# First attention by chunks of 64: the second chunk attends the first through a score block instead of a carried state

## Chip, cores and metric

One core of one Trainium2 chip. The metric is the device time of one execution in microseconds, lower is better.

## What is computed

Two layers over x of 16 sequences x 256 tokens x 128 features. Each layer normalizes the rows, runs an attention and a mixture of experts on them, and adds attention x silu(experts) to x. The change lies in the first attention, a gated linear attention with 4 heads, keys of 128 and values of 32, in chunks of 64 tokens:

```
G = cumsum(gk within a chunk)             # log gates, gk = log_sigmoid(..)/16
qg = q*exp(G)*scale ; k_intra = k*exp(-G) ; kg = k*exp(G_last - G)
A = tril(qg k_intra^T) ; o = A v          # inside a chunk
o += qg S ; S = S*exp(G_last) + kg^T v    # state carried to the next chunk
```

The output o is then divided by its root mean square per head, gated, and projected by Wo. The result of the attention multiplies that of the first experts later.

## The kernel before

The tokens are handled in 16 blocks b of 256, one sequence each. A sequence is laid out as two halves u of 128 columns, and its columns are ordered 63..0, 64..127 within a tile of 128 tokens (ORDER): chunk 0 of the tile runs backwards and chunk 1 forwards, and the gate sums start at their common border. So the two chunks of 64 of one tile share one reference point, and 128 tokens take part in one masked score block; only from the first 128 tokens to the second is something carried (the text calls these halves the first and the second chunk).

The work on a block is a pipeline of ticks t, written out by hand for every engine in `gla(t, part)` with part 0, 1, 2 (all five engines walk the same schedule, `walk`). In tick t block t gets its gates (`gate_out`, `gate_logs`, `gate_sigmoids`), block t-1 its exponentials (`decays`: ACT writes bufP and bufN, L1005 and L1006), values, queries and keys (`queries_keys` L501 to L503, `scaled` L1550 and L1552), block t-2 its scores, block t-3 its outputs (L551, L554), block t-4 its mean, gate and projection (`output_means` L559, `output_gates` L1922, `gated` L1558, `project` L567, `attended` L1045).

Ticks 1 to 6 run beside the scatter of the normalized rows to `xs` by GpSimd's indirect DMAs (L1877, 64 of them in 18 parts; each part waits for a product of TensorE that `part_multiplied` names) and the preparation of the expert weights (`w1`, L606, L607, L963, L1485). Then come 19 expert groups g of the first layer: `turn` (L616, L1082, L1589), the experts' up products (L661 to L663), tanh (`gates0`, L1093), product (`hidden0`, L1598), down product (`down0`, L675), bias (`biased0`, L1608) and indirect stores (L1896). TICKS says which group carries which tick: (7, 8, 9, 0, 10, 11, 0, 12, 13, 0, 14, 15, 0, 16, 0, 17, 18, 19, 0), 0 for none. A group runs: turn of group g+1, `gla(t, 0)`, experts parts 0 and 1, `gla(t, 1)`, down product, `gla(t, 2)`.

What each engine has in the parts that matter, in program order:

- TensorE part 0: `output_means(t-4)`, `gate_out(t)`, `key_values(t-3)` (L539). Part 1: `outputs(t-3)` from tick 7 on, `keys_turned(t-2)` (L517: four transposes of 128x128), `scores(t-2)` (L528, L529), `gate_in(t+1)` (L475), `values(t-1)` (L509). Part 2: `queries_keys(t-1)`, `project(t-4)`.
- ScalarE part 0: `outputs_scale` (L1039, L1041), `gate_logs` (L990 to L994). Part 1: `keys_moved(t-2)` (L1019), `decays(t-1)`, `gate_moved(t+1)` (L978), `values_moved(t-1)` (L1025). Part 2: `outputs_squared`, `chunk_hi`, `attended(t-4)`. Table loads are L881.
- VectorE part 0: `states(t-3)` (L1535), `gated`, the scan of `decays(t-1)` (L1514); before tick 7 the scan comes first. Part 1: `masked(t-2)` (L1527), `gate_low(t+1)` (L1496), `chunk_lo(t-1)` (L1518), `gate_sigmoids(t)` (L1505, L1506). Part 2: `scaled(t-1)`.
- GpSimd part 1: `chunk_ends(t-1)` (L1916), a 128x4 product that waits for both exponentials; and `output_gates(t-4)`, in part 0 from tick 7 on.

Before, the carried part goes: the scaled keys of the first 128 tokens are transposed on TensorE (`keys_turned`), copied out by ScalarE (`keys_moved`), multiplied with the values to a 128x32 state per head (`key_values`), scaled by `ends` on VectorE (`states`), and in `outputs` the state multiplies the queries of the second 128 tokens.

Matrix products go to a ring of four PSUM banks (`Ring`, `bank`): a product takes the next bank and first waits for the signal given for the bank's use four takes earlier. In a group with a tick the order of takes is: turn, state product, four for the experts (b0, a0, b1, a1), turned keys, two score banks, gate product, values, down product, four for queries and keys, projection. b0 and b1 are freed by the tanh rows, a0 and a1 by `hidden0`. An fp32 matmul shows as two records of the trace.

Of the kernel before, what the change touches and what calls it, by code (L numbers as in the profile page):

```python
# [68 lines left out]
def build(nc, A, out):  # L69
    with ExitStack() as ctx:  # L70
# [7 lines left out]
        def sig(name, per=1):  # L78
            return Sig(ctx.enter_context(nc.semaphore(name)), per)
# [55 lines left out]
        bufE = [sb(1040) for _ in range(2)]  # L135
        bufK, bufKT = [sb(1024) for _ in range(2)], [sb(512) for _ in range(2)]
        bufP, bufN = sb(1040), sb(1040)
# [3 lines left out]
        bufV = [sb(256) for _ in range(3)]  # L141
        bufS = [sb(128) for _ in range(2)]
        ends = [sb(4) for _ in range(4)]
        osq_all = sb(512)
# [101 lines left out]
        gate2, gate2_ln, decay = sig("gate2", 2), sig("gate2_ln", 4), sig("decay", 5)  # L246
        pn, p_ends = sig("exp_decay", 2), sig("chunk_ends")
# [3 lines left out]
        kt, kt_moved = sig("k_turned"), sig("k_turned_moved")  # L251
        att, att_masked = sig("att", 2), sig("att_masked", 2)
        kv, state = sig("kv"), sig("state")
        o_mm, o_sq, o_mean, o_rs, o_gate, o_y = sig("o_mm"), sig("o_squared"), sig("o_mean"), sig("o_rs", 2), sig("o_gate"), sig("o_gated")
# [134 lines left out]
        def _(eng):  # L389
# [121 lines left out]

            def keys_turned(b):
                k4 = bufK[b % 2].rearrange("p (h c) -> p h c", h=4)
                k = bank(("kt", b), kt_moved.at(b))
                eng.wait_ge(*qk_mul.at(b))
                for h in range(4):
                    i = eng.transpose(k[:, 128 * h:128 * h + 128], k4[:, h, 0:128], ident)  # L517
                i.then_inc(kt.sem, 1)

            def scores(b):  # L520

                q4 = bufQ[b % 3].rearrange("p (h c) -> p h c", h=4)
                k4 = bufK[b % 2].rearrange("p (h c) -> p h c", h=4)
                for u in range(2):
                    k, n = bank(("att", b, u), att_masked.at(b, u)), slice(128 * u, 128 * u + 128)
                    early, late = slice(128 * u, 128 * u + 64), slice(128 * u + 64, 128 * u + 128)
                    for h in range(4):
                        mm(k[0:64, 128 * h:128 * h + 128], k4[:, h, early], q4[:, h, n])  # L528
                        i = mm(k[64:128, 128 * h + 64:128 * h + 128], k4[:, h, late], q4[:, h, late])  # L529
                    i.then_inc(att.sem, 1)  # L530

            def key_values(b):

                KT, v = bufKT[b % 2], bufV[b % 3]
                k = bank(("kv", b), state.at(b))
                eng.wait_ge(*kt_moved.at(b))
                eng.wait_ge(*v_moved.at(b))
                for h in range(4):
                    i = mm(k[:, 32 * h:32 * h + 32], KT[:, 128 * h:128 * h + 128], v[:, 32 * h:32 * h + 32])  # L539
                i.then_inc(kv.sem, 1)  # L540

            def outputs(b):

                v, S, A4, o = bufV[b % 3], bufS[b % 2], bufAT[b % 2], o_banks[b % 2]
                q4 = bufQ[b % 3].rearrange("p (h c) -> p h c", h=4)
                if b > 1:
                    eng.wait_ge(*o_y.at(b - 2))
                for u in range(2):
                    eng.wait_ge(*att_masked.at(b, u))
                    for h in range(4):  # L550
                        mm(o[32 * h:32 * h + 32, 128 * u:128 * u + 128], v[:, 128 * u + 32 * h:128 * u + 32 * h + 32], A4[:, u, h, :], start=(u == 0), stop=(u == 0))  # L551
                eng.wait_ge(*state.at(b))
                for h in range(4):
                    i = mm(o[32 * h:32 * h + 32, 128:256], S[:, 32 * h:32 * h + 32], q4[:, h, 128:256], start=False)  # L554
                i.then_inc(o_mm.sem, 1)
# [14 lines left out]
            def gla(t, part):  # L570
                def at(b):
                    return 0 <= b < NB
                if part == 0:
                    if at(t - 4):
                        output_means(t - 4)
                    if at(t):
                        gate_out(t)
                    if at(t - 3):
                        key_values(t - 3)
                elif part == 1:  # L580
                    if at(t - 3) and t >= OUTPUTS_EARLY:
                        outputs(t - 3)
                    if at(t - 2):
                        keys_turned(t - 2)
                        scores(t - 2)
# [290 lines left out]
        def _(eng):  # L876
# [119 lines left out]
            def decays(b):  # L996
# [3 lines left out]
                if b >= 1:  # L1000
                    eng.wait_ge(*qk_mul.at(b - 1))
                    eng.wait_ge(*p_ends.at(b - 1))
                else:
                    eng.wait_ge(*set_pool.at(0, 11))
# [9 lines left out]

            def keys_moved(b):
                eng.wait_ge(*kt.at(b))
                if b >= 2:
                    eng.wait_ge(*kv.at(b - 2))
                act(bufKT[b % 2], bank_of["kt", b][:, :], ACT.Copy).then_inc(kt_moved.sem, 1)  # L1019

# [26 lines left out]
            def gla(t, part):  # L1047
# [7 lines left out]
                elif part == 1:  # L1055
                    if at(t - 2):
                        keys_moved(t - 2)
                    if at(t - 1):
# [216 lines left out]
        def _(eng):  # L1275
# [252 lines left out]

            def states(b):
                kv_, S = (a.rearrange("p (h d) -> p h d", h=4) for a in (bank_of["kv", b][:, 0:128], bufS[b % 2]))  # L1530
                eng.wait_ge(*kv.at(b))
                eng.wait_ge(*p_ends.at(b))
                if b > 1:
                    eng.wait_ge(*o_mm.at(b - 2))
                tt(S, kv_, bc(ends[b % 4], 2, [128, 4, 32]), ALU.mult).then_inc(state.sem, 1)  # L1535

# [23 lines left out]
            def gla(t, part):  # L1560
                def at(b):
                    return 0 <= b < NB
                if part == 0:
                    if at(t - 1) and t < OUTPUTS_EARLY:
                        decays(t - 1)
                    if at(t - 3):
                        states(t - 3)
                    if at(t - 4) and t >= OUTPUTS_EARLY:
# [14 lines left out]
                elif at(t - 1):  # L1583
                    scaled(t - 1)


# [200 lines left out]
        def _(eng):  # L1787
# [111 lines left out]
            def experts0(g, part):  # L1899
                if part == 0 and g >= 2:  # L1900
                    t = TICKS[g]
                    eng.wait_ge(*(kv.at(t - 3) if 0 < t < 19 else up[0].at(g, 1) if g < 18 else down[0].at(17)))
                    store(0, g - 2, 1)
                if part == 0 and g + 1 < GROUPS[0]:
                    ids(0, g + 1)
                if part == 2 and g >= 1:
                    store(0, g - 1, 0)
                    if g == 18:
                        store(0, 17, 1)

            def chunk_ends(b):
                P, N = (a.rearrange("p (h u s) -> p h u s", h=4, u=2) for a in (bufP, bufN))
                eng.wait_ge(*pn.at(b))
                if b >= 4:
                    eng.wait_ge(*state.at(b - 4))
                tt(ends[b % 4], P[:, :, 0, 128], N[:, :, 1, 64], ALU.mult).then_inc(p_ends.sem, 1)  # L1916

# [220 lines left out]
```

## Time and profile before

| | us |
|---|---|
| runs shown, median of 3 | 987.14 (986.79 to 999.11) |
| profiled execution, its own time | 995.33 |
| its span, first to last instruction | 993.3 |
| TensorE busy | 738.5 (74%) |
| VectorE busy | 646.1 (65%) |
| ScalarE busy | 616.1 (62%) |
| GpSimd busy | 453.9 (46%) |

Busy times are parts of the span and overlap each other. The rows below are of the profiled execution. Its time is 8 us above the median of the runs, so differences are to be taken against its own time. Ticks 1 to 6 lie between about 46 and 157 us of it, the groups with ticks 7 to 19 between 157 and 387 us; the rest, to 993 us, is the second layer, with the joining of the first.

### The profile page before, as it was taken

The page shows a single profiled execution, that of the slowest core. Times are in us where ns is not written, and L with a number is a line of the kernel's source. Part 1 is how long each engine was busy: PE and PEld are TensorE (multiplying, and loading weights), DVE is VectorE, ACT ScalarE, POOL GpSimd, SP SyncE. Part 2 cuts the span into 40 slices and gives each one's busy share as a digit, 9 for nine tenths or more (in the row PEclk, how much of TensorE's full clock was granted, in tenths as well). Part 3 has the DMA queues.
Part 4 walks back from the last instruction along what each step waited for, and adds up shares of the span by engine and source line. Part 5 has one row for each costly group of instructions (what it writes and reads, how often), then busy time and mean ns, then how long its engine had stood idle before and what let it go on. Part 6 is the DMA issues. An engine that isn't in the chain of part 4 may idle for free.

```text
span 993.3 us, 21325 instructions
## 1 busy us (share of the span) xinstructions
PE 738.5 (74%) x8182; PEld 573.3 (58%) x8182; DVE 646.1 (65%) x1190; ACT 616.1 (62%) x1139; POOL 453.9 (46%) x484
## 2 busy tenths in 40 slices
PE   6756776989898992466954788687978888888650
PEld 4535555878887892344642445456756766766540
DVE  5765655766666643777567554575677777687647
ACT  5653455766667462675641434475778878878775
POOL 4485763242443454100004665223566666756632
PEclk8777879999999996678885777698999999999985
DMA  9811222011111113400003321300111111110054
GB/s 310 304 45 47 62 64 58 20 50 31 47 47 39 46 42 108 115 1 2 1 1 119 121 85 60 86 13 23 30 39 41 34 39 39 42 36 26 19 158 118
DMA packets 62357, 63.81 MB, mean 64 GB/s; under 512 B 7378, under 2 KB 52322, under 8 KB 62132
## 3 DMA queue, kind: packets, MB, share of 16 engines
q1 hardware_dynamic: 53300, 44.02, 15.1%
q0 software_dynamic: 8960, 18.43, 5.7%
q8 instruction: 68, 1.11, 0.5%
q14 instruction: 29, 0.24, 0.1%
HBM read 31.88 MB, written 30.55 MB: 63 GB/s over the span
## 4 chain that ended last, share of the span: by engine, by line
PE 33%; ACT 19%; DVE 17%; issue 16%; POOL 9%; DMA 2%; another core or an unknown queue 2%; SPq 0%; ACTq 0%; POOLq 0%; DVEq 0%
POOL xs L1877 6%; ACT arena L1220 4%; PE bank L721 4%; ACT L881 3%; PE bank L786 3%; PE bank L675 3%; PE bank L798 2%; PE bank L528 2%; POOL ys L1896 2%; DVE arena L1644 2%; DVE arena L1737 2%; ACT arena L1121 2%; DVE arena L1624 1%; DVE arena L1642 1%
## 5 line engine op out<-in xcount | busy, mean ns | idle before, releaser
L1896 POOL DMA_INDIRECT ys<-arena x152 | 172.3, 1134 | 178.4 <-ACT arena L1149 56.3
L1877 POOL DMA_INDIRECT xs<-arena x128 | 131.3, 1026 | 77.1 <-issue 33.5
L1220 ACT ACTIVATE arena<-bank 128x512 f32<-128x512 f32 x192 | 99.1, 600 | 83.6 <-PE bank L786 62.1
L1737 DVE TENSOR_REDUCE arena<-bank 128x2 bf16<-128x512 f32 (+1 forms) x192 | 119.0, 682 | 41.9 <-PE bank L759 37.8
L661 PE MATMUL bank<-arena 128*128 128x128 bf16 x608 | 105.9, 220 | 6.4 <-DVE arena L1589 3.3
L662 PE MATMUL bank<-arena 128*128 128x128 bf16 x608 | 105.9, 220 | 0.0
L663 PE MATMUL bank<-arena 128*128 128x128 bf16 x608 | 105.9, 220 | 0.0
L881 ACT ACT_TABLE_LOAD x72 | 92.4, 1283 | 1.3
L1725 DVE SCALAR_TENSOR_TENSOR arena<-arena,bank 128x512 bf16<-128x512 bf16 x64 | 46.0, 746 | 71.2 <-ACT arena L1193 68.0
L721 PE MATMUL bank<-arena 128*128 128x256 f32 x256 | 67.2, 410 | 0.9 <-issue 0.9
L661 PEld LDWEIGHTS bank<-arena 128*128 x608 | 60.2, 99 | 9.6 <-issue 6.5
L662 PEld LDWEIGHTS bank<-arena 128*128 x608 | 59.8, 98 | 0.3
L663 PEld LDWEIGHTS bank<-arena 128*128 x608 | 59.6, 98 | 0.0
L1828 POOL TENSOR_TENSOR arena<-arena 128x4 f32<-128x4 f32 x16 | 16.2, 1010 | 87.9 <-DVE arena L1323 80.7
L721 PEld LDWEIGHTS bank<-arena 128*128 128x128 f32 x256 | 50.7, 208 | 9.3 <-issue 2.6
L691 PE MATMUL bank<-arena 128*128 x320 | 44.1, 296 | 14.5 <-POOL arena L1942 11.7
L1942 POOL TENSOR_TENSOR arena<-arena 128x1024 f32<-128x1024 f32 x19 | 44.7, 2355 | 20.4 <-ACT arena L1130 19.0
L691 PEld LDWEIGHTS bank<-arena 128*128 128x128 f32 x320 | 42.1, 211 | 17.5 <-issue 17.0
L756 PE MATMUL bank<-arena 32*128 32x256 bf16 (+1 forms) x512 | 22.8, 273 | 38.5 <-DVE arena L1725 14.9
L501 PE MATMUL bank<-arena 128*128 128x256 bf16 x128 | 37.9, 296 | 11.8 <-DVE arena L1518 7.5
L1193 ACT ACTIVATE arena<-bank 128x512 bf16<-128x512 f32 x64 | 36.6, 609 | 16.1 <-PE bank L721 15.6
L1937 POOL TENSOR_TENSOR arena<-arena 128x512 f32<-128x512 f32 x40 | 40.6, 1035 | 10.7 <-DVE arena L1644 10.7
(236 smaller groups left out, 2063.9 us busy)
## 6 DMA issues: line engine op xcount, KB each, us to landing
xs<-arena SPq DMA_DIRECT2D x19, 516.0 KB, 7.2
arena<-xs SPq DMA_DIRECT2D x38, 258.0 KB
arena<-ys SPq DMA_DIRECT2D x32, 256.0 KB, 5.1
arena<-in_MF SPq DMA_DIRECT2D x8, 512.0 KB
ys<-arena POOLq DMA_INDIRECT x152
arena<-in_x SPq DMA_DIRECT2D x8, 256.0 KB, 5.7
arena<-in_W SPq DMA_DIRECT2D x8, 256.0 KB
xs<-arena POOLq DMA_INDIRECT x128
```

The source lines that it names most:

```text
L661: mm(o, hi, b[:, 0, c4], stop=False)
L662: mm(o, hi, b[:, 1, c4], start=False, stop=False)
L663: i = mm(o, lo, b[:, 0, c4], start=False)
L691: i = mm(k[:, 128 * j:128 * j + 128], tb[g % 2][:, h0:h0 + 128], D, start=(c == 0), stop=(c == 1))
L721: j = mm(k[:, 256 * z:256 * z + 256], Wqk[:, c:c + 128], xnT[:, 256 * b:256 * b + 256])
L881: eng.preload_act_table_set(name)
L1220: act(PT[kt_][:, i, gs[0]:gs[0] + len(gs), :], bank_of["s2", b, n, i][:, :].rearrange("p (g q) -> p g q", q=w), ACT.Exp, scale=8 ** -0.5). ...
L1725: stt(T, hiT[n % 2], low_of[n // 2], bank_of["qk1", b, n][:, :], ALU.mult, ALU.add).then_inc(m_qk_moved.sem, 1)
L1737: red(negM[b % 2][:, u, 32 * i + gs[0]:32 * i + gs[0] + len(gs)], kv_, op=ALU.max, negate=True).then_inc(m_max.sem, 1)
L1877: eng.indirect_dma_start(xs[l][:, :], bass.IndirectOffsetOnAxis(ap=slot_i[l][:, m:m + 1], axis=0), xrow[:, t, :], None).then_inc(rows_move ...
L1896: eng.indirect_dma_start(ys[l][:, :], bass.IndirectOffsetOnAxis(ap=yid[g % 4][:, j:j + 1], axis=0), y[:, 128 * j:128 * j + 128], None).the ...
L1942: tt(T, T, U, ALU.mult).then_inc(f1_h.sem, 1)
```

## The change

`keys_turned`, `keys_moved`, `key_values`, `states` and `chunk_ends` go. Instead VectorE, behind `scaled(t-1)` in part 2, multiplies the keys of the first 128 tokens with `ends` (`keys_shifted`: a 128x4 product, then a 128x512 product into bufKX). TensorE multiplies them with the queries of the second 128 tokens to a third score bank, behind the two of `scores`; ScalarE copies it to bufX, where it copied the turned keys before; `outputs` multiplies it with the values. The scores inside a tile, formed before by two products of 64 keys (128 and 64 queries wide), are formed by one of 128 keys and 128 queries. The ring takes: the state product's bank is gone, and so is the turned keys'; the cross scores take one behind the score banks. ScalarE's exponentials wait for the new `ends` product instead of GpSimd's. The store on GpSimd that waited for the state product waits for `output_means(t-4)`.

```diff
-        bufK, bufKT = [sb(1024) for _ in range(2)], [sb(512) for _ in range(2)]
+        bufK, bufKX, bufX = [sb(1024) for _ in range(2)], [sb(512) for _ in range(2)], [sb(512) for _ in range(2)]
...
-        bufS = [sb(128) for _ in range(2)]
-        ends = [sb(4) for _ in range(4)]
+        ends = [sb(4) for _ in range(2)]
...
@@ TensorE
-            def keys_turned(b):
-                k4 = bufK[b % 2].rearrange("p (h c) -> p h c", h=4)
-                k = bank(("kt", b), kt_moved.at(b))
-                eng.wait_ge(*qk_mul.at(b))
-                for h in range(4):
-                    i = eng.transpose(k[:, 128 * h:128 * h + 128], k4[:, h, 0:128], ident)
-                i.then_inc(kt.sem, 1)
...
-                    early, late = slice(128 * u, 128 * u + 64), slice(128 * u + 64, 128 * u + 128)
+                    if u == 0:
+                        eng.wait_ge(*qk_mul.at(b))
                     for h in range(4):
-                        mm(k[0:64, 128 * h:128 * h + 128], k4[:, h, early], q4[:, h, n])
-                        i = mm(k[64:128, 128 * h + 64:128 * h + 128], k4[:, h, late], q4[:, h, late])
+                        i = mm(k[:, 128 * h:128 * h + 128], k4[:, h, n], q4[:, h, n])
                     i.then_inc(att.sem, 1)
-
-            def key_values(b):
-
-                KT, v = bufKT[b % 2], bufV[b % 3]
-                k = bank(("kv", b), state.at(b))
-                eng.wait_ge(*kt_moved.at(b))
-                eng.wait_ge(*v_moved.at(b))
+                k = bank(("cross", b), cross_moved.at(b))
+                eng.wait_ge(*k_shifted.at(b))
                 for h in range(4):
-                    i = mm(k[:, 32 * h:32 * h + 32], KT[:, 128 * h:128 * h + 128], v[:, 32 * h:32 * h + 32])
-                i.then_inc(kv.sem, 1)
+                    i = mm(k[:, 128 * h:128 * h + 128], bufKX[b % 2][:, 128 * h:128 * h + 128], q4[:, h, 128:256])
+                i.then_inc(cross.sem, 1)
...
+                eng.wait_ge(*v_moved.at(b))
                 for u in range(2):
...
-                eng.wait_ge(*state.at(b))
+                eng.wait_ge(*cross_moved.at(b))
                 for h in range(4):
-                    i = mm(o[32 * h:32 * h + 32, 128:256], S[:, 32 * h:32 * h + 32], q4[:, h, 128:256], start=False)
+                    i = mm(o[32 * h:32 * h + 32, 128:256], v[:, 32 * h:32 * h + 32], bufX[b % 2][:, 128 * h:128 * h + 128], start=False)
...
-                    if at(t - 3):
-                        key_values(t - 3)
...
-                        keys_turned(t - 2)
                         scores(t - 2)
@@ ScalarE
-                    eng.wait_ge(*p_ends.at(b - 1))
+                    eng.wait_ge(*k_shifted.at(b - 1, 0))
...
-            def keys_moved(b):
-                eng.wait_ge(*kt.at(b))
+            def crossed(b):
+                eng.wait_ge(*cross.at(b))
                 if b >= 2:
-                    eng.wait_ge(*kv.at(b - 2))
-                act(bufKT[b % 2], bank_of["kt", b][:, :], ACT.Copy).then_inc(kt_moved.sem, 1)
+                    eng.wait_ge(*o_mm.at(b - 2))
+                act(bufX[b % 2], bank_of["cross", b][:, :], ACT.Copy).then_inc(cross_moved.sem, 1)
...
-                        keys_moved(t - 2)
+                        crossed(t - 2)
@@ VectorE
-            def states(b):
-                kv_, S = (a.rearrange("p (h d) -> p h d", h=4) for a in (bank_of["kv", b][:, 0:128], bufS[b % 2]))
...
-                tt(S, kv_, bc(ends[b % 4], 2, [128, 4, 32]), ALU.mult).then_inc(state.sem, 1)
+            def keys_shifted(b):
+
+                k4, kx = (a.rearrange("p (h c) -> p h c", h=4) for a in (bufK[b % 2], bufKX[b % 2]))
+                P, N = (a.rearrange("p (h u s) -> p h u s", h=4, u=2) for a in (bufP, bufN))
+                tt(ends[b % 2], P[:, :, 0, 128], N[:, :, 1, 64], ALU.mult).then_inc(k_shifted.sem, 1)
+                eng.wait_ge(*k_shifted.at(b, 0))
+                eng.wait_ge(*qk_mul.at(b))
+                if b >= 2:
+                    eng.wait_ge(*cross.at(b - 2))
+                tt(kx, k4[:, :, 0:128], bc(ends[b % 2], 2, [128, 4, 128]), ALU.mult).then_inc(k_shifted.sem, 1)
...
-                    if at(t - 3):
-                        states(t - 3)
...
                     scaled(t - 1)
+                    keys_shifted(t - 1)
@@ GpSimd
-                    eng.wait_ge(*(kv.at(t - 3) if 0 < t < 19 else up[0].at(g, 1) if g < 18 else down[0].at(17)))
+                    eng.wait_ge(*(o_mean.at(t - 4) if t else up[0].at(g, 1) if g < 18 else down[0].at(17)))
...
-            def chunk_ends(b):
-                P, N = (a.rearrange("p (h u s) -> p h u s", h=4, u=2) for a in (bufP, bufN))
-                eng.wait_ge(*pn.at(b))
...
-                tt(ends[b % 4], P[:, :, 0, 128], N[:, :, 1, 64], ALU.mult).then_inc(p_ends.sem, 1)
...
-                if part == 1 and 0 <= t - 1 < NB:
-                    chunk_ends(t - 1)
```

## Rows read from the trace of the kernel before

**Rows 1.** By stage: window and its length, busy us of each engine, granted clock, DMA
```profile
46.00:157.00 111.00, 73.72 (x566) 54.04 (x566) 67.60 (x124) 52.62 (x89) 75.58 (x79) 0.77 0.17 53
157.00:387.00 230.00, 197.48 (x2430) 180.78 (x2430) 139.78 (x224) 146.91 (x226) 92.64 (x114) 0.95 0.15 42
```

**Rows 2.** Waits of 160 to 390 us: engine line, releaser, total us, times, longest
```profile
ACT arena L1045 <- PE bank L567: 35.4, 12, 4.2
```

**Rows 3.** TensorE in tick 9: start us, us, engine, line, operation, [idle before]
```profile
200.10 0.66 PE L517 MATMUL bank<-arena 128*128 128x128 f32 x4 [1.40 <-ACT arena L1093]
200.82 0.32 PE L528 MATMUL bank<-arena 128*64 128x128 f32 x1
...
202.71 0.66 PE L475 MATMUL bank<-arena 128*80 128x128 f32 x4
...
203.66 1.95 PE L675 MATMUL bank<-arena 128*128 128x128 f32 x16
205.44 0.27 PE L501 MATMUL bank<-arena 128*128 128x256 bf16 x1
...
208.06 0.61 PE L567 MATMUL bank<-arena 128*128 128x128 f32 x4
...
209.24 0.22 PE L661 MATMUL bank<-arena 128*128 128x128 bf16 x1
```

**Rows 4.** ScalarE in tick 9, the same columns
```profile
199.44 1.09 ACT L1093 ACTIVATE arena<-bank 128x512 f32<-128x512 f32 x2
200.79 0.60 ACT L1019 ACTIVATE arena<-bank 128x512 f32<-128x512 f32 x1 [0.26 <-PE bank L517]
...
203.41 0.38 ACT L978 ACTIVATE arena<-bank 80x256 bf16<-80x256 f32 x1
...
208.71 0.38 ACT L1045 ACTIVATE arena<-bank 128x256 f32<-128x256 f32 x1 [3.89 <-PE bank L567]
```

**Rows 5.** VectorE in tick 9
```profile
200.08 1.29 DVE L1598 SCALAR_TENSOR_TENSOR arena<-arena,bank 128x512 f32<-128x512 f32 x2 [1.60 <-ACT arena L1093]
...
203.82 0.42 DVE L1496 TENSOR_TENSOR arena<-bank,arena 16x256 bf16<-16x256 f32 x1 [0.26 <-ACT arena L978]
...
204.27 0.43 DVE L1518 TENSOR_TENSOR arena<-arena 128x256 bf16<-128x256 f32 x1
...
207.86 1.28 DVE L1552 TENSOR_TENSOR arena<-bank,arena 128x512 f32<-128x512 f32 x2
```

**Rows 6.** TensorE elsewhere: tick 7's first query product; tick 10's state product and turn
```profile
174.29 0.27 PE L501 MATMUL bank<-arena 128*128 128x256 bf16 x1 [1.03 <-DVE arena L1518]
...
215.13 0.98 PE L539 MATMUL bank<-arena 128*128 128x32 f32 x8
...
222.41 1.11 PE L517 MATMUL bank<-arena 128*128 128x128 f32 x4 [2.82 <-ACT arena L1093]
```

**Rows 7.** Granted clock in ticks 9 and 10, columns as in rows 1
```profile
200.10:205.40 5.30, 5.23 (x60) 4.83 (x61) 4.25 (x8) 4.29 (x8) 0.20 (x1) 1.00 0.22 50
222.40:230.40 8.00, 7.99 (x60) 7.33 (x61) 4.42 (x9) 4.90 (x9) 0.20 (x1) 0.63 0.15 35
```

**Rows 8.** Groups of 100 to 470 us: count, busy us, mean ns of one
```profile
L1535 DVE TENSOR_TENSOR arena<-bank,arena 128x128 f32<-128x128 f32 x15 | 4.4, 291 | 3.8 <-PE bank L539 2.7 <-issue 1.1
```

**Rows 9.** Lines L1673 and L1323: count, duration ns min/median/max, first and last start
```profile
L1673 DVE TENSOR_TENSOR arena<-arena x8: 681/684/685, 396.6 to 447.4; 128x512 f32<-128x512 f32 x8
...
L1323 DVE TENSOR_SCALAR arena<-arena x8: 160/163/382, 403.5 to 477.4; 128x4 f32<-128x4 f32 x8
```

**Rows 10.** GpSimd in the scatter stage: its wait in total, then rows in time
```profile
POOL arena L1916 <- ACT arena L1006: 12.2, 4, 5.2
...
154.75 0.95 POOL L1877 DMA_INDIRECT xs<-arena  x1 [0.30 <-issue]
```

**Rows 11.** TensorE where the scatter stage ends
```profile
155.73 0.38 PE L607 MATMUL bank<-arena 128*128 128x512 bf16 x1
160.57 2.04 PE L616 MATMUL bank<-arena 128*128 128x128 f32 x8 [4.46 <-DMA arena<-xs]
```

More of the change, by code:

```diff
@@ L246, in build @@
         gate2, gate2_ln, decay = sig("gate2", 2), sig("gate2_ln", 4), sig("decay", 5)
-        pn, p_ends = sig("exp_decay", 2), sig("chunk_ends")
+        pn, k_shifted = sig("exp_decay", 2), sig("k_shifted", 2)
         xq_hi, xq_lo = sig("chunk_hi"), sig("chunk_lo")
@@ L250, in build @@
         vv, v_moved = sig("v"), sig("v_moved")
-        kt, kt_moved = sig("k_turned"), sig("k_turned_moved")
+        cross, cross_moved = sig("att_cross"), sig("att_cross_moved")
         att, att_masked = sig("att", 2), sig("att_masked", 2)
-        kv, state = sig("kv"), sig("state")
         o_mm, o_sq, o_mean, o_rs, o_gate, o_y = sig("o_mm"), sig("o_squared"), sig("o_mean"), sig("o_rs", 2), sig("o_gate"), sig("o_gated")
@@ L525, in scores @@
                     k, n = bank(("att", b, u), att_masked.at(b, u)), slice(128 * u, 128 * u + 128)
-                    early, late = slice(128 * u, 128 * u + 64), slice(128 * u + 64, 128 * u + 128)
+                    if u == 0:
+                        eng.wait_ge(*qk_mul.at(b))
                     for h in range(4):
-                        mm(k[0:64, 128 * h:128 * h + 128], k4[:, h, early], q4[:, h, n])
-                        i = mm(k[64:128, 128 * h + 64:128 * h + 128], k4[:, h, late], q4[:, h, late])
+                        i = mm(k[:, 128 * h:128 * h + 128], k4[:, h, n], q4[:, h, n])
                     i.then_inc(att.sem, 1)
-            def key_values(b):
-                KT, v = bufKT[b % 2], bufV[b % 3]
-                k = bank(("kv", b), state.at(b))
-                eng.wait_ge(*kt_moved.at(b))
-                eng.wait_ge(*v_moved.at(b))
+                k = bank(("cross", b), cross_moved.at(b))
+                eng.wait_ge(*k_shifted.at(b))
                 for h in range(4):
-                    i = mm(k[:, 32 * h:32 * h + 32], KT[:, 128 * h:128 * h + 128], v[:, 32 * h:32 * h + 32])
-                i.then_inc(kv.sem, 1)
+                    i = mm(k[:, 128 * h:128 * h + 128], bufKX[b % 2][:, 128 * h:128 * h + 128], q4[:, h, 128:256])
+                i.then_inc(cross.sem, 1)
             def outputs(b):
-                v, S, A4, o = bufV[b % 3], bufS[b % 2], bufAT[b % 2], o_banks[b % 2]
-                q4 = bufQ[b % 3].rearrange("p (h c) -> p h c", h=4)
+                v, A4, o = bufV[b % 3], bufAT[b % 2], o_banks[b % 2]
                 if b > 1:
                     eng.wait_ge(*o_y.at(b - 2))
+                eng.wait_ge(*v_moved.at(b))
                 for u in range(2):
@@ L1527, in masked @@
                     eng.copy_predicated(bufAT[b % 2][:, u], bc(maskA, 1, [128, 4, 128]), bank_of["att", b, u].rearrange("p (h c) -> p h c", h=4)).then_inc(att_masked.sem, 1)
-            def states(b):
-                kv_, S = (a.rearrange("p (h d) -> p h d", h=4) for a in (bank_of["kv", b][:, 0:128], bufS[b % 2]))
[L1531 to L1534, printed above, removed]
-                tt(S, kv_, bc(ends[b % 4], 2, [128, 4, 32]), ALU.mult).then_inc(state.sem, 1)
+            def keys_shifted(b):
[7 more added lines that the diff above has]
+                tt(kx, k4[:, :, 0:128], bc(ends[b % 2], 2, [128, 4, 128]), ALU.mult).then_inc(k_shifted.sem, 1)
             def scaled(b):
@@ L1909, in experts0 @@
                         store(0, 17, 1)
-            def chunk_ends(b):
-                P, N = (a.rearrange("p (h u s) -> p h u s", h=4, u=2) for a in (bufP, bufN))
-                eng.wait_ge(*pn.at(b))
-                if b >= 4:
-                    eng.wait_ge(*state.at(b - 4))
-                tt(ends[b % 4], P[:, :, 0, 128], N[:, :, 1, 64], ALU.mult).then_inc(p_ends.sem, 1)
             def output_gates(b):
```

## The prediction, made before the run

> **What bounds the kernel now.** I read the time by stage first. The change touches the stretch up to 387 us and nothing behind it: the scatter stage (ticks 1 to 6, 46 to 157 us) and the expert groups with ticks 7 to 19 (157 to 387 us). In the second TensorE is busy 197.5 of 230 us, VectorE 140, ScalarE 147 [rows 1]: no engine is full, so the order of one tick decides. The waits say how: ScalarE stands 35.4 us, 12 times, before `attended` for the projection on TensorE [rows 2]. I then lined up one tick on three engines. In tick 9 ScalarE ends its first tanh at 199.44 + 0.60 = 200.04 [rows 4]; TensorE stood idle 1.40 us for it and then works without a gap: keys turned from 200.10, scores from 200.82, gate product 202.71, `down0` 203.66, queries and keys 205.44, projection 208.06 [rows 3]. ScalarE answers at 208.71, after 3.89 us idle [rows 4], and has its long row of gate logarithms before the next tanh. So the tick is a loop: a TensorE half (tanh to projection), then a ScalarE half (projection to tanh). A delay in either lengthens the tick; idle time of ScalarE inside the TensorE half is free, until it is used up.
>
> Inside the TensorE half runs a side chain that must be done before the queries: ScalarE's copy of the turned keys (200.79), two exponentials, the gate copy (203.41) [rows 4]; VectorE's `gate_low` (203.82) and `chunk_lo`, done at 204.27 + 0.43 = 204.70 [rows 5]. The queries start at 205.44 [rows 3]: the side chain has 0.7 us to spare, 0.6 after the 0.1 us that a wait takes. In tick 7, which has no `down0`, it has none: the queries there waited 1.03 us for VectorE [rows 6].
>
> **Part by part, per tick, at full clock.**
> TensorE. Scores: 16 records of 128x64 weights with the 128x64 ones beside them, 200.82 to 202.71, 1.9 us [rows 3]. Whole blocks are 16 records of 128x128 weights by 128 columns; `down0` issues 16 such in 1.78 us (203.66 to 205.44) [rows 3], 0.11 each. So the scores cost the same, since the two half-width products already ran side by side: between -0.1 and, if the halves had been worth something, +0.2; I take 0. The turn goes (200.10 to 200.76), and with it the gap until the scores; the cross scores come: 8 records, 0.9 us. The state product goes, 8 records from 215.13, 0.98 us [rows 6], but it lies in the ScalarE half, ahead of the 1.4 to 2.8 us that TensorE idles [rows 3, 6]: worth nothing there. The output products keep their count (v for the state, the moved cross scores for the queries): 0.
> ScalarE. A 128x512 copy for a 128x512 copy, 0.60 us both [rows 4]: 0. But the old copy waited for four turns, the new one waits for the scores and the cross scores. All three are queued behind the same tanh: first block 200.10 to 200.98 (its ring bank is now the one that the first tanh frees), second to 201.86 (bank free when VectorE's 0.69 us product ends, 200.77 from rows 5: no wait), cross to 202.74, last record's end about 202.9. The copy moves from 200.79 to 202.9: **+2.1 us**. Queued behind it on ScalarE are both exponentials and the gate copy; behind that on VectorE `gate_low`, `chunk_lo`, the sigmoids, all of `scaled`.
> VectorE. The state multiply goes, 0.29 us [rows 8]. Added: one 128x4 product, between 0.16 (a 128x4 operation) and 0.4, and one 128x512 product from the arena, 0.68 [rows 9]: 0.85 to 1.1, I take 0.9, net +0.6. It stands behind `scaled`, ahead of the next tick's `lo`, `gated` and scan, and VectorE idled 1.60 us for the tanh behind these [rows 5]. That wait hides it. If that cover were gone it would cost up to 0.6 x 10 = 6 us.
> The Trainium skill (SBUF — State Buffer, "Who interferes with whom") says that a VectorE instruction with both inputs in SBUF contends with a GpSimd instruction that reads SBUF, and that one blocks the other for its whole length; the new product has both inputs there, the state multiply had one in PSUM. By that rule some ticks would pay one more 0.7 us on VectorE. `chunk_lo` too has two such inputs and took 0.43 us in the row shown [rows 5], not stretched; GpSimd's reading operation is short and rare, so the sum leaves this out.
>
> Now the consequence. The side chain ends at 204.70 + 2.1 = 206.8 instead of 204.70; the queries start at 206.9 instead of 205.44: **+1.4 us** on the tick. VectorE's `scaled` is behind the side chain alone and moves the full 2.1: its end goes from 207.86 + 1.28 = 209.14 [rows 5] to 211.2. The next experts start at 209.24 [rows 3], because one of their ring banks is freed by that end. Where the next group has a tick, mean and gate products stand between (0.9 us) and cover the difference. Where it has none, the experts wait, and the loss is 2.1. Five ticks are of that kind (9, 11, 13, 15, 16), and tick 7 has no slack: 6 x 2.1 = 12.6. Ticks 8, 10, 12, 14: 4 x 1.4 = 5.6. In tick 10 the clock is 0.63 [rows 7] and everything on TensorE takes up to twice as long: the copy comes 4.1 us later, but ScalarE had idled 2 us there; about the same 1.2 to 1.4 remains. Sum **+18.2 us**. Ends of this term: if only TensorE's own surplus counted (0.9 + the shorter gap = 0.15 per tick) +1.5; if every tick paid 2.1 and the VectorE addition as well, 10 x 2.7 = +27. I take 18, since each step of it stands in rows.
> Tick 18: no exponentials; the state product there is on the chain: -0.8.
> GpSimd. `chunk_ends` and its wait for the exponentials go. In the groups nothing there is late. In the scatter stage it held up the scatters for 12.2 us [rows 10]. Without it the scatters run until the next of their own waits (gate, value and query products, `output_gates`); followed wait by wait the last starts 5.5 us before 154.75 [rows 10]. But TensorE has its own work there until 155.73 + 0.38 = 156.1, and starts the first turn at 160.57 after 4.46 us idle [rows 11]: at most -4.4. Against it, the later copy: ticks 4 and 5 reach it after TensorE is done anyway; tick 3 pays 0 to 3, tick 6 some 1.6. Between -4.4 and +1.5; I take **-2.4**. The store of expert rows that waited for the state product waits for the output mean, a microsecond earlier: 0.
>
> Sum: 18.2 - 0.8 - 2.4 = **+15.0 us**. The profiled execution took 995.3 us (span 993.3), 8 above the median of the runs shown, 987.1. On it the forecast is 1010; on the median **1002 us**, 1.5% slower.
>
> **Rivals.**
> *The delay is absorbed.* ScalarE's 3.89 us idle before `attended` speaks for it, and TensorE loses 1.6 us of work against 0.9. Against it: the idle lies behind the side chain, not ahead of it. If half the steps have cover that I don't see: +9 - 3.2 = +6, down to 0; 987 to 993.
> *The scatters decide: faster.* One mechanism: GpSimd's wait in ticks 3 to 6 goes and the first turn comes 4.4 us earlier, the scatters' stall being the real bound; with the tick chains not late (bank waits that I took for bound being loose) 1.5 - 0.8 - 4.4 = -3.7, and should the stage follow the full 12.2 us, -11.5: 976 to 983. It decides once the group ticks lose less than 5 us together. Against it are rows 11: TensorE's own 156.1.
> *The clock.* After 2.82 us idle tick 10 ran with a granted clock of 0.63 (part of it at the 1.2 GHz level); tick 9, after 1.40 us, at 1.00 (2.4 GHz) [rows 3, 6, 7]. The change takes 0.8 us of work from just before that idle and adds 1.4 us of idle ahead of the queries. A slow tick needs 222.41 to 230.40 for what takes 200.10 to 205.44 otherwise: 2.65 us more. If the seven ticks that now run at full clock fall, 7 x 2.65 = 18.5 more: 1020. Against it: in tick 7 the 1.03 us wait did not lower it, whose first query record took 0.27 us as in tick 9 [rows 3, 6].
> The Trainium skill (TensorE: Matmul & The Clock Gate, Part 1) holds that the default state is throttled and activity releases the throttle; by it more idle can only bring this rival nearer, and the rows above agree in direction.
>
> **How the numbers follow.** Forecast 0.52, absorbed 0.18, clock 0.20, scatters 0.10. The range reaches from the absorbed case to short of the full clock case: 987 to 1016. Slower by over 2% (above 1007, about what a measurement can tell from no change is those 2%, 20 us): the clock case 0.20 and the upper tail of the forecast 0.07, so 0.27. Faster by over 2% (below 967): 0.01. Within: 0.72.
>
> **What would show it.** Right: the ScalarE copy waits 2 us more behind the tanh; the queries wait for `chunk_lo` in every tick, 1 us or more; tick 9 to 10 grows by 2.1, tick 8 to 9 by 1.4; the first turn after the scatters comes some 2 us earlier; VectorE's idle before the tanh product shrinks but stays. Wrong: queries that start directly behind `down0`; a granted clock near 0.6 in ticks that had 1.00; a stretch behind the stores (387 us on) that changes its length.

## The result and the profile after

The changed kernel takes 1002.4 us (median of 4 runs), against 989.3 us for the kernel before in the same series: a ratio of 1.0138, with a 95% interval of 1.0097 to 1.0178. In a later series of six runs it was 1.0165 (1.0127 to 1.0204). The forecast was 1002, in a range of 987 to 1016; as a difference it was 15.0 us, and the medians differ by 13.0 here and by 16.8 in the later series.

| profiled executions, us | own time | first turn after the scatters | from it to the last down product | from that to the end of the span |
|---|---|---|---|---|
| before | 995.3 | 160.6 | 216.8 | 616.0 |
| before, second profile (e1) | 993.0 | 157.8 | 216.6 | 616.7 |
| after | 996.2 | 150.3 | 230.9 | 613.1 |
| after, second profile (e2) | 1003.7 | 154.1 | 234.1 | 613.7 |

By the states on record the first profiled execution of before is a slow one and the other three are fast, so the second pair is the one to compare. In it the group stage (from the first turn to the last down product) is 17.5 us longer, the scatter stage ends 3.8 us earlier, and the stretch behind is 3.0 us shorter; in the first pair it is 14.1, 10.3 and 2.9. These are starts of the rows of `turn` and `down0`; the last column is the span less both.

TensorE in tick 9 of the changed kernel answers to [rows 3]; the columns are start us, us, engine, line, operation, idle before:

```profile
194.32 2.05 PE L519 MATMUL bank<-arena 128*128 128x128 f32 x16 [2.21 <-ACT arena L1075]
196.21 1.06 PE L524 MATMUL bank<-arena 128*128 128x128 f32 x8
197.10 0.60 PE L473 MATMUL bank<-arena 128*80 128x128 f32 x4
...
197.98 1.95 PE L657 MATMUL bank<-arena 128*128 128x128 f32 x16
201.13 0.27 PE L499 MATMUL bank<-arena 128*128 128x256 bf16 x1 [1.20 <-DVE arena L1500]
...
205.53 0.22 PE L643 MATMUL bank<-arena 128*128 128x128 bf16 x1 [0.58 <-DVE arena L1537]
```

Scores and cross scores are 24 records in 2.8 us (194.32 to 197.10). The 16 of the scores take 1.89 us (194.32 to 196.21), as the half-width ones did before (200.82 to 202.71). Then there is a gap that wasn't there: the queries (L499) wait 1.20 us for VectorE's L1500, `chunk_lo`. In tick 7 they wait 2.99 us, where it was 1.03 [rows 6]. The experts (L643), which had followed the projection and turn closely, now wait for the end of VectorE's `scaled`.

ScalarE in the same tick, for [rows 4]:

```profile
193.66 1.09 ACT L1075 ACTIVATE arena<-bank 128x512 f32<-128x512 f32 x2
197.30 0.60 ACT L1001 ACTIVATE arena<-bank 128x512 f32<-128x512 f32 x1 [2.55 <-PE bank L524]
...
199.71 0.37 ACT L960 ACTIVATE arena<-bank 80x256 bf16<-80x256 f32 x1
...
204.43 0.39 ACT L1027 ACTIVATE arena<-bank 128x256 f32<-128x256 f32 x1 [3.51 <-PE bank L552]
```

The copy of the cross scores (L1001) comes 3.64 us behind the tanh's start (before: 1.35) after 2.55 us idle, the gate copy 6.05 (before: 3.97), the projection's copy 10.77 (before: 9.27).

VectorE, for [rows 5]:

```profile
194.30 1.29 DVE L1582 SCALAR_TENSOR_TENSOR arena<-arena,bank 128x512 f32<-128x512 f32 x2 [1.60 <-ACT arena L1075]
...
200.11 0.42 DVE L1478 TENSOR_TENSOR arena<-bank,arena 16x256 bf16<-16x256 f32 x1 [2.97 <-ACT arena L960]
200.56 0.42 DVE L1500 TENSOR_TENSOR arena<-arena 128x256 bf16<-128x256 f32 x1
...
204.15 1.28 DVE L1537 TENSOR_TENSOR arena<-bank,arena 128x512 f32<-128x512 f32 x2
205.34 0.15 DVE L1515 TENSOR_TENSOR arena<-arena 128x4 f32<-128x4 f32 x1
205.53 0.69 DVE L1520 TENSOR_TENSOR arena<-arena 128x512 f32<-128x512 f32 x1
```

`chunk_lo` ends 200.56 + 0.42 - 193.66 = 7.32 us behind the tanh's start, 5.26 before. The last two rows are the new work, 0.15 and 0.69 us, behind `scaled`. The 1.60 us idle ahead of the tanh product (L1582) is the same as before: the new work is hidden.

The waits of the group stage, for [rows 2] (engine line, releaser, us in total, times, longest):

```profile
ACT arena L1001 <- PE bank L524: 35.1, 11, 5.1
...
ACT arena L1027 <- PE bank L552: 27.8, 11, 3.5
DVE arena L1478 <- ACT arena L960: 25.7, 8, 3.8
...
PE bank L499 <- DVE arena L1500: 11.3, 8, 3.0
```

ScalarE's wait for the cross scores is 35.1 us (5.6 us for the turned keys before, in waits not shown there). `gate_low` on VectorE and the queries on TensorE now wait behind it; the wait for the projection has shrunk from 35.4 to 27.8 us, since a part of ScalarE's idle was spent earlier.

### The profile page after: what moved, and what is told of

The parts are those of the page before. It is cut to its first block, busy times and chain, and to the rows that moved or that the text cites. A ratio compares the mean times of both kernels' runs of the same rounds, so it can differ in the third digit from the quotient of the medians.

```text
span 994.3 us, 20675 instructions
## 1 busy us (share of the span) xinstructions
PE 721.1 (73%) x7862; PEld 561.2 (56%) x7862; DVE 651.7 (66%) x1206; ACT 612.5 (62%) x1139; POOL 452.9 (46%) x468
## 4 chain that ended last, share of the span: by engine, by line
PE 24%; ACT 16%; DVE 14%; issue 10%; another core or an unknown queue 3%; POOL 2%; DMA 1%; SPq 0%; ACTq 0%; DVEq 0%
ACT arena L1202 5%; PE bank L703 4%; PE bank L780 3%; PE bank L768 3%; ACT L863 2%; PE bank L673 2%; DVE arena L1628 2%; DVE arena L1721 2%; ACT arena L1103 2%; PE bank L782 1%; DVE arena L1608 1%; DVE arena L1626 1%; PE bank L761 1%; DVE arena L1709 1%
## 5 line engine op out<-in xcount | busy, mean ns | idle before, releaser
L1880 POOL DMA_INDIRECT ys<-arena x152 | 172.0, 1131 | 230.9 <-DVE arena L1592 102.9
L643 PE MATMUL bank<-arena 128*128 128x128 bf16 x608 | 105.7, 220 | 8.5 <-DVE arena L1573 3.7
L643 PEld LDWEIGHTS bank<-arena 128*128 x608 | 59.1, 97 | 12.1 <-issue 6.2
L703 PE MATMUL bank<-arena 128*128 128x256 f32 x256 | 64.6, 398 | 0.9 <-issue 0.9
L519 PE MATMUL bank<-arena 128*128 128x128 f32 x256 | 38.2, 310 | 28.8 <-ACT arena L1075 25.3
L519 PEld LDWEIGHTS bank<-arena 128*128 128x128 f32 x256 | 35.4, 219 | 34.4 <-ACT arena L1075 28.3
L499 PE MATMUL bank<-arena 128*128 128x256 bf16 x128 | 36.4, 284 | 24.1 <-DVE arena L1500 17.8
L703 PEld LDWEIGHTS bank<-arena 128*128 128x128 f32 x256 | 48.8, 201 | 8.5 <-issue 2.6
L738 PE MATMUL bank<-arena 32*128 32x256 bf16 (+1 forms) x512 | 22.9, 273 | 38.5 <-DVE arena L1709 15.6
L673 PEld LDWEIGHTS bank<-arena 128*128 128x128 f32 x320 | 40.3, 203 | 17.1 <-issue 16.6
```

The lines of the kernel that those rows point to most:

```text
L519: i = mm(k[:, 128 * h:128 * h + 128], k4[:, h, n], q4[:, h, n])
L643: mm(o, hi, b[:, 0, c4], stop=False)
L673: i = mm(k[:, 128 * j:128 * j + 128], tb[g % 2][:, h0:h0 + 128], D, start=(c == 0), stop=(c == 1))
L703: j = mm(k[:, 256 * z:256 * z + 256], Wqk[:, c:c + 128], xnT[:, 256 * b:256 * b + 256])
L1880: eng.indirect_dma_start(ys[l][:, :], bass.IndirectOffsetOnAxis(ap=yid[g % 4][:, j:j + 1], axis=0), y[:, 128 * j:128 * j + 128], None).the ...
```

## The experiments

The experiments ran in three series of four kernels (e1 to e4, e5 to e8, e9 to e12), each on a chip of its own with runs of the kernel before beside them; ratios are to these. In the second series the kernel before took 946.8 us instead of 987 to 988. In the profiles of e5 to e8 the scatter stage ended at 142 to 144 us (149 in e7), and the stretch behind the last down product took 585 to 588 us instead of 613 to 621. So only ratios and stages are compared across series. The kernel before was profiled twice, both times outside the second and third series.

**e1, e2: both kernels again**, unchanged, for second profiles.

> The kernel before, unchanged, for a second profile. If the first one is typical, the first turn after the scatters starts near 160.6 us, the last down product 216.8 us later, and what lies behind takes 616 us. The medians differ by 13 us where the two profiled executions differ by 1, so some stretch of the first profile must be untypical: my guess is the stretch behind the down products (616 in it, 8 to 12 us less here). The rival: the scatter stage, which then ends near 152 here and gained nothing by the change.

> The changed kernel, unchanged, for a second profile. Ratio to before 1.010 to 1.018. The theory (copy held up behind scores and cross scores) has the last down product 228 to 233 us after the first turn, ticks at full clock of 17.1 us from projection copy to projection copy. The rival (clock) has most of the surplus in ticks at a granted clock under 0.8.

Measured: before 989.8 us, 1.0004 (0.9976 to 1.0032); after 1003.6 us, 1.0165. The guess about the stretch behind was wrong: it took 616.7 us, as in the first profile (616.0). Both profiled executions of before (995.3, and a span of 991.1) are slower than its median, and the first one of the changed kernel (996.2) is the fastest of its four. The two pairs of spans put the change at 1.0 and 10.7 us (994.3 - 993.3, 1001.8 - 991.1), the medians at 13 to 17. Which stage is shorter in the median execution stays open.

**e3: the copy behind the exponentials.** ScalarE part 1 of the changed kernel:

```diff
+                    if at(t - 1):
+                        decays(t - 1)
                     if at(t - 2):
                         crossed(t - 2)
-                    if at(t - 1):
-                        decays(t - 1)
```

> The changed kernel with ScalarE's copy of the cross scores put behind the two exponentials instead of ahead of them. The theory: the exponentials start right behind the tanh again, the copy fits into ScalarE's wait for the gate product, the tick at full clock falls from 17.1 to about 15.5 us, the group stage to 215 to 219 us, the time by 10 to 14 us: 0.996 to 1.003 of before. The rival that the cost is TensorE's cross product or VectorE's shift product leaves it within 3 us of the changed kernel.

Measured: 991.8 us, 1.0048 (1.0019 to 1.0077), 11.9 us less than e2. ScalarE in one tick:

```profile
192.64 1.09 ACT L1075 ACTIVATE arena<-bank 128x512 f32<-128x512 f32 x2
193.61 1.07 ACT L987 ACTIVATE arena<-arena 128x1040 f32<-128x1040 f32 x1
...
197.90 0.60 ACT L1001 ACTIVATE arena<-bank 128x512 f32<-128x512 f32 x1 [2.26 <-PE bank L524]
198.40 0.37 ACT L960 ACTIVATE arena<-bank 80x256 bf16<-80x256 f32 x1
```

The exponentials (L987) start 0.97 us behind the tanh's start, the copy (L1001) fits ahead of the gate copy (L960), as expected. The group stage fell from 234.1 to 222.8 us, short of the 215 to 219 that I expected. This very tick took 17.3 us, not 15.5, at a granted clock of 0.90. So did two more regular ticks (17.2 and 17.3 us), and a fourth took 16.9; one (269.0 to 284.7 us) took 15.7 at 1.00. Something else was left.

**e4: the 128x4 product back on GpSimd** (`chunk_ends` with its wait for the exponentials; `keys_shifted` waits for it).

> The changed kernel with the 128x4 product back on GpSimd, with its wait for the exponentials. The theory: the wait of 10 to 14 us in the scatter stage is back and the first turn comes 3 to 10 us later than in the changed kernel (near 154 to 160), the group stage is the same within 1 us: slower than the changed kernel by 3 to 10 us, 1.017 to 1.024 of before. The rival that the earlier end of the scatter stage was chance: no difference, 1.014.

Measured: 1006.6 us, 1.0178 (1.0141 to 1.0216), 3.0 us above e2; in the scatter stage GpSimd waits 6.8 us for the exponentials again (10 to 14 expected), the first turn starts at 155.2 and the group stage takes 234.1, as in e2. The time is at the small end of what was expected, and the intervals of e2 and e4 overlap, so that the product is worth something there is likely, not shown.

**e5, e11: that product alone on VectorE in the kernel before.**

```diff
@@ VectorE
...
                     scaled(t - 1)
+                    chunk_ends(t - 1)
@@ GpSimd
...
-                if part == 1 and 0 <= t - 1 < NB:
-                    chunk_ends(t - 1)
```

> The kernel before, with the 128x4 product alone moved from GpSimd to VectorE behind the scaling (the state product and all else as before). In the profiles the scatter stage from tick 2's lower half of x to the first turn takes 66 us before, 61 with the changed kernel and the product on GpSimd, 55 with the changed kernel. The theory that GpSimd's wait is worth about 6 of these 11 us by itself: 59 to 62 here, the group stage 217 as before, the time 0.993 to 0.998 of before. The rival that TensorE's own work in that stage is the bound, as the prediction had it: 64 to 66, and 1.000.

> The same kernel as e5 (before, the 128x4 product alone moved to VectorE). In the call of e5 the scatters stood nowhere for the instruction stream and the move was worth nothing (1.0005). The theory: it is worth 3 to 7 us (0.993 to 0.997) only where before has 8 to 12 us of that wait, as in its profiles of the first call; where the scatter stage ends near 143 us again, 0. The rival that the wait is never worth anything, since TensorE's own work is the bound: 1.000 whatever the stage takes.

Measured: e5 1.0005 (0.9983 to 1.0028), first turn at 143.2; e11 983.1 us, 0.9955 (0.9919 to 0.9991), first turn at 152.4. From `chunk_lo` of tick 2 to the first turn, the measure of the expectation, e5 took 59.1 us and e11 57.7. So the move is worth 4.4 us in the series with the long scatter stage and nothing in the one with the short. That the 4.4 us lie in that stage is likely, since its end comes at 152.4 instead of 157.8 to 160.6 us, but not shown: e11's group stage is shorter too (213.3 us against 216.6 and 216.8), and the kernel before has no profile in its series. TensorE at the end of that stage in e11, for [rows 11]:

```profile
151.12 0.38 PE L607 MATMUL bank<-arena 128*128 128x512 bf16 x1
152.43 0.63 PE L616 MATMUL bank<-arena 128*128 128x128 f32 x4 [0.93 <-DMA arena<-xs]
```

TensorE's own work there (the w1 product, L607) ends at 151.5, 4.6 us earlier than in [rows 11], though nothing of it was changed.

**e7: one wait added to the kernel before.** `keys_moved` also waits for the scores (`eng.wait_ge(*att.at(b))`); no work is added.

> The kernel before, with one wait added: ScalarE's copy of the turned keys also waits for the scores. No work is added. The theory that the order on ScalarE is the cost: the copy starts 1.9 us later, the ticks at full clock take 17.0 instead of 15.6 us, the group stage 227 to 231 instead of 217, the time 1.010 to 1.014 of before. If the changed kernel loses by its own new work: 1.000 to 1.003.

Measured: 970.1 us, 1.0239 (1.02 to 1.0278); ScalarE in a tick:

```profile
195.40 1.09 ACT L1094 ACTIVATE arena<-bank 128x512 f32<-128x512 f32 x2
198.84 0.60 ACT L1020 ACTIVATE arena<-bank 128x512 f32<-128x512 f32 x1 [2.35 <-issue]
...
201.25 0.37 ACT L978 ACTIVATE arena<-bank 80x256 bf16<-80x256 f32 x1
...
205.98 0.38 ACT L1046 ACTIVATE arena<-bank 128x256 f32<-128x256 f32 x1 [3.51 <-PE bank L567]
```

The copy (L1020) starts 3.44 us behind the tanh's start, the projection's copy 10.58, and the tick takes 17.0 us: the signature of the changed kernel without one instruction of its work. The group stage took 232.8 us, 17.5 more than e5's 215.3 in the same series, where 10 to 14 were expected. 7.1 of the 17.5 lie ahead of tick 7's projection copy, in a stretch at a granted clock of 0.69 (1.00 in e5); the other 10.4 are the longer ticks. The scatter stage was 5.7 us longer too. These two put the ratio above what I expected, and why one added wait brings them stays open.

**e8: half-width scores in the changed kernel.**

```diff
+                    early, late = slice(128 * u, 128 * u + 64), slice(128 * u + 64, 128 * u + 128)
...
-                        i = mm(k[:, 128 * h:128 * h + 128], k4[:, h, n], q4[:, h, n])
+                        mm(k[0:64, 128 * h:128 * h + 128], k4[:, h, early], q4[:, h, n])
+                        i = mm(k[64:128, 128 * h + 64:128 * h + 128], k4[:, h, late], q4[:, h, late])
```

> The changed kernel with each score block formed by the two half-width products again. The prediction's term of 0 for whole blocks: the same as the changed kernel within 1.5 us, tick at full clock 17.1 us, 1.014 to 1.018 of before. If whole blocks had gained something, 1 to 4 us slower.

Measured: 969.5 us, 1.0236 (1.02 to 1.0272), above the 1.014 to 1.018 that I expected. The two regular ticks at a granted clock of 1.00 took 17.2 and 17.3 us, and the scores in the first of them 1.89 us, both as with whole blocks. But the group stage took 237.6 us, 3.5 to 6.7 more than with whole blocks: two more regular ticks ran at 0.91 and took 18.8 us each, and no tick with an empty group reached 1.00. The changed kernel has no run in this series, so whether the half-width products have a part in that stays open; the 0 for whole blocks is shown for the tick at full clock alone. Beside it e7, the kernel before with one wait more, took 970.1 us: the changed kernel with these products costs as much as that wait.

**e6, e10, e9, e12: unread products against the clock.** In ticks 7 to 16, behind `outputs` and ahead of the wait for the tanh, TensorE gets 8 products into columns that the mean overwrites later:

```diff
                         outputs(t - 3)
+                        if t < 17:
+                            for _ in range(8):
+                                mm(o_banks[(t - 3) % 2][:, 256:512], trib, Wqk0[:, 0, 0:256])
```

e6 and e10 are this on e3; e9 is e3 again, beside e10; e12 is this on the changed kernel.

> The kernel with ScalarE's copy behind the exponentials, and 8 products of 128x256 bf16 that nobody reads on TensorE ahead of each tick's wait for the tanh (ticks 7 to 16), in the place of the work that the change took away. The clock theory: five ticks that took 17.2 us at a granted clock of 0.90 take 15.7 at 1.00, the group stage falls from 222.8 to 215 to 218 us, the time by 4 to 8 us, to 0.994 to 0.999 of before. The rival that the remaining 6 us are the cross product's own time: no change, or slower by up to 1 us a tick, 1.005 to 1.012.

> The same kernel as e3 (the copy behind the exponentials, no filling), beside e10 so that the filling is the only difference between two runs of one call. The clock theory: some ticks of 17.2 us at a granted clock of 0.90 are here again, the group stage takes 221 to 224 us, 6 to 9 more than in e10, and the time is 0.4 to 0.9% above that of e10. If the fall between e3 and e6 came with the other call and not with the filling: ticks of 15.7 us here too, and no difference.

> The same kernel as e6. The clock theory: all ticks with their next at 15.7 us and 1.00, the group stage 213 to 216 us, 1 to 3 us less than with the kernel before; 0.994 to 1.000 of before.

> The changed kernel, its order kept, with the 8 unread products ahead of each tick's wait for the tanh. The theory has two costs in it: the order (1.55 us in a tick at full clock, 2.1 with an empty group behind) and a clock part of 3 to 7 us in ticks under 1.00. The filling takes the second alone: ticks 17.1 to 17.3 us, with an empty group 24.4, group stage 228 to 231 us, 1.010 to 1.015 of before. If the clock were the whole cost, the group stage would fall to 217 and the time to that of before.

Measured: e6 946.9 us, 0.9996 (0.9973 to 1.0019), group stage 213.3. In the third series e9 992.4 us, 1.0047 (1.0019 to 1.0074), 222.6; e10 981.9 us, **0.9945 (0.9915 to 0.9976)**, 214.7; e12 997.0 us, 1.0104 (1.0060 to 1.0148), 227.8. Two ticks of e9 by window (its length, busy us of TensorE, its weight loads, VectorE, ScalarE, GpSimd, granted clock, DMA):

```profile
168.60:184.30 15.70, 13.49 (x160) 12.65 (x159) 11.95 (x21) 12.26 (x20) 2.20 (x4) 1.00 0.08 19
184.30:201.40 17.10, 14.89 (x160) 14.05 (x159) 11.99 (x21) 10.95 (x18) 5.89 (x7) 0.90 0.12 33
```

The same two of e10:

```profile
168.60:184.30 15.70, 14.46 (x168) 13.34 (x167) 11.95 (x21) 12.25 (x19) 2.17 (x4) 1.00 0.07 18
184.30:200.00 15.70, 14.47 (x168) 13.35 (x167) 11.98 (x21) 10.96 (x19) 5.94 (x7) 1.00 0.14 39
```

With the filling (L568) TensorE is busy on 0.97 us more in the first and 0.42 us less in the second, and no regular tick of e10 is below 1.00 (two of its three ticks with an empty group still ran at 0.93). What was 2.21 us idle is now 1.23:

```profile
188.66 0.40 PE L539 MATMUL bank<-arena 128*32 128x128 f32 x8
189.00 1.05 PE L568 MATMUL bank<-arena 128*128 128x256 bf16 x8
191.28 2.05 PE L519 MATMUL bank<-arena 128*128 128x128 f32 x16 [1.23 <-ACT arena L1078]
```

e10 beats both kernels: by 0.55% the one before. The cross scores have no visible part in that: e11, the kernel before with the 128x4 product moved, gained 0.45% in the same series, and the intervals overlap. e6 in the second series was the same as before. The kernel before with the unread products was not tried.

## Why the prediction was right, and where not

**The side chain: right.** The copy was forecast to come 2.1 us later; it came 2.29 later (3.64 - 1.35), and the end of `chunk_lo` 2.06. Start of the queries: +1.4 forecast, 7.47 - 6.00 = 1.47 measured. End of `scaled` and start of the next experts: +2.1 forecast, 205.53 - 193.66 = 11.87 against 9.80, 2.07 measured. e3 and e7 show the cause from both sides: the order taken back in the changed kernel removes 11.9 us (11.3 of the group stage), and the order alone put on the kernel before brings the 17.0 us ticks.

**Ticks 15 and 16: wrong, 4.2 us too many.** The step "Five ticks are of that kind (9, 11, 13, 15, 16)" held two that don't have the side chain: there is no block 16, so neither `gate_moved` nor `gate_low` stands between ScalarE's exponentials and `chunk_lo`. In tick 15 the queries follow `down0` without a wait:

```profile
326.54 1.95 PE L657 MATMUL bank<-arena 128*128 128x128 f32 x16
328.32 0.27 PE L499 MATMUL bank<-arena 128*128 128x256 bf16 x1
```

Without these the term is 14.0. Measured: four regular stretches between projection copies grew from 15.5 or 15.6 to 17.0 to 17.2 us, 6.4 together. One with an empty group takes 24.4 against 22.3 at a clock of 1.00 (the latter in e11), 2.1 each for the three of them. Up to tick 7's projection copy it is 2.2 to 2.9. The stretch that ends in tick 15 grew by 0.2, and behind it nothing did: some 15 us in all. The -0.8 for tick 18 didn't come as forecast: from tick 15's projection copy to the last down product it is 49.8 us before and 49.5 to 49.6 after, so -0.3.

**The clock: the rival's loss is not clear in the changed kernel, and shown behind e3.** One regular stretch and the three with an empty group in the changed kernel, by window:

```profile
187.20:204.40 17.20, 13.78 (x160) 12.59 (x160) 11.97 (x21) 10.85 (x18) 5.85 (x6) 1.00 0.11 32
204.40:228.80 24.40, 19.04 (x227) 17.55 (x228) 14.62 (x25) 15.32 (x23) 9.90 (x11) 1.00 0.16 45
246.00:272.10 26.10, 20.72 (x228) 19.24 (x228) 14.70 (x25) 15.33 (x24) 9.89 (x11) 0.93 0.15 42
289.30:316.20 26.90, 21.66 (x227) 20.17 (x227) 14.63 (x25) 15.29 (x23) 9.91 (x11) 0.87 0.14 40
```

The regular one and the first long one ran at 1.00, the others at 0.93 and 0.87 and took 1.7 and 2.5 us more, 4.2 together. The kernel before has such losses too; its first stretch with an empty group, and the same one in e11:

```profile
208.70:233.70 25.00, 22.05 (x249) 20.30 (x248) 14.59 (x24) 15.57 (x24) 10.35 (x13) 0.86 0.16 44
199.80:222.10 22.30, 19.27 (x249) 17.82 (x248) 14.42 (x25) 15.57 (x24) 9.93 (x12) 1.00 0.18 49
```

With two more it loses 5.6 us by this measure. In the second pair it is 4.4 us in e1 and 7.1 in e2 (1.5, 2.6, 1.4 and 1.6). So the clock made the group stage 1.4 us shorter in the first pair and 2.7 longer in the second, and what is left of its 14.1 and 17.5 us, 15.5 and 14.8, is the order. e12 agrees: the filling took 3 to 6 us from the changed kernel's group stage (230.9 and 234.1, to 227.8) and left the order. Of the seven ticks at full clock that the rival wanted to fall none did in the first profile of the changed kernel, and one in e2 (18.6 us at 0.91). Yet in e3 four regular ticks and in e9 three fell to 0.90, which no regular tick of the kernel before did. They have the same 2.21 us idle ahead of the scores as those at 1.00; in the second tick of e9 shown above the clock was 0.50, the 1.2 GHz level, from 191.2 us, where that idle ends, to 193.0. What decides there between 0.90 and 1.00 stays open; that the unread products, with less idle behind them, keep it at 1.00 is shown by e9 and e10. That agrees with the rule of the Trainium skill (TensorE: Matmul & The Clock Gate, Part 1) that activity releases the throttle.

**The scatter stage: sign right, size wrong.** Forecast -2.4, "at most -4.4", from TensorE's own end at 156.1. The two pairs of profiles have -3.8 and -10.3. The cap holds in the second pair alone; the other profiles of the first and third series with the product on VectorE (e3, e9 to e12) end the stage at 149.9 to 152.5 us, 5 to 8 us ahead of e1. In the changed kernel:

```profile
148.61 0.38 PE L589 MATMUL bank<-arena 128*128 128x512 bf16 x1
150.31 0.63 PE L598 MATMUL bank<-arena 128*128 128x128 f32 x4 [1.32 <-DMA arena<-xs]
```

TensorE's own work ends at 149.0 now, and in e11 at 151.5: the row that I took for an independent bound moves too. I costed GpSimd's wait as if the rest stood still. Of the gain e4 puts 3 us and e11 4.4 us on GpSimd's wait, with the reserves named there. Why TensorE's work comes earlier with it, and what the rest is (the ring with one take less is the candidate), was not tried.

**Hidden work: right.** VectorE's products took 0.15 and 0.69 us, and 1.60 us idle were still there behind them; I had expected it to shrink. All 16 large products took 0.693 to 0.696 us, so nothing stretched them. The rule on two inputs in SBUF (the Trainium skill, SBUF — State Buffer, "Who interferes with whom") cost nothing here, but it was not put to the test either: in this profile no product ran beside a computing instruction of GpSimd, only beside the issue of its indirect DMAs. The state product's 0.98 us were worth nothing in time, as forecast; whether they were worth something for the clock, which I had only in the rival, no run takes by itself.

**The sum.** The measured 1002.4 us lie within 0.4 us of the forecast, and that is luck in part. The kernel before stood 2.2 us higher in the result's runs than in those that I had (989.3, 987.1), and the errors have opposite signs: 4.2 too much for ticks 15 and 16, some 1 too little in the other ticks, up to 2.7 too little for the clock, 1 to 8 too little gain at the scatters. One sign that I had called wrong came too: the stretch behind is 3 us shorter in both pairs. Unchanged there, it took 613 to 621 us in the profiles of the first and third series, so I don't put it on the change. The median agrees better than the profiled executions, which differ by 1 and 11 us; part of that is unexplained.

## What to carry to other kernels

Before an operand of a pipelined tick is replaced, look at what is queued behind its consumer: an equal copy that waits 2 us longer delays everything behind it on that in-order engine, and the fix is one line, to put it behind the work that is already ready. A stage's idle time helps only if it lies ahead of the delayed step. Where TensorE idles 2 us ahead of a burst in every tick, look at the granted clock tick by tick; 8 unread products a tick won 10 us back here. And check a bound by asking whether it would move too.

## What was not expected of the hardware

1.0 us of unread products a tick, ahead of a wait, made regular ticks 15.7 us at a granted clock of 1.00 where some had taken 16.9 to 17.3 at 0.90. Between e9 and e10 it was 10.5 us of the whole time, 7.9 of them in the group stage. And the kernel before took 946.8 us on one chip and 987 to 988 us on two others. In the profiles of all kernels the difference is in the scatter stage (142 to 149 against 150 to 161 us for its end) and in the stretch behind (585 to 588 against 613 to 621; granted clock there 0.87 in e5, 0.84 in the kernel before and e11). Its cause is open.
